# Three fillers between small on-chip buffers, in a post-norm transformer block

## The reference

```python
qkv = einsum('bsd,ed->bse', x, w_qkv) + b_qkv
scores = einsum('bhqd,bhkd->bhqk', q, k) / sqrt(32) + causal
out = einsum('bhqk,bhkd->bhqd', softmax(scores), v)
x = layernorm(x + einsum('bsd,ed->bse', out, w_out) + b_out)
Wg = (gate_w - 128) * gate_scale[:, None]        # Wu and Wd likewise
h = silu(einsum('bsh,ih->bsi', x, Wg)) * einsum('bsh,ih->bsi', x, Wu)
x = layernorm(x + einsum('bsi,hi->bsh', h, Wd))
```

## The kernel before, in words

| Buffers | Address modulo 256 |
|---|---|
| ident, x_tok, xT_hi, xT_lo, z_tok | 128 |
| w_stage; attT_hi, attT_lo, v_tok, q_sb, k_sb, wT_hi, wT_lo; hid_hi, hid_lo, gateT, upT, downT | 224 |
| inv_wide, attT | 160 |
| probs0 to probs3, probsT | 64 |

## Time and profile before

### The profile page before, as it was taken

How to read it: one execution, slowest core, us unless ns; L and a number is a source line. 1 busy time by engine, 2 the same in 40 slices (tenths; PEclk the granted TensorE clock), 3 DMA queues, 4 the chain that set the end, 5 groups by cost and what they waited for, 6 DMA issues and landing times.

```text
span 789.9 us, 11953 instructions
## 1 busy us (share of the span) xinstructions
PE 753.0 (95%) x4480; PEld 571.7 (72%) x4480; DVE 395.0 (50%) x1006; ACT 387.3 (49%) x914; POOL 128.3 (16%) x148
## 2 busy tenths in 40 slices
PE   7998899999999999999899999899999999999993
PEld 6776576776777676776578887688887888788882
DVE  3755666667567665667542222543226332453236
ACT  3754766666676666667646564422324222322220
POOL 0000111315131050302742233200000000000001
PEclk9999999999999999999999999899999999999997
DMA  9201422335422454312679944501110020000201
GB/s 315 85 1 28 134 60 74 81 81 139 149 62 59 115 149 134 81 37 52 138 131 196 265 146 146 175 14 40 67 54 0 13 82 11 0 1 27 80 1 55
DMA packets 59719, 68.67 MB, mean 87 GB/s; under 512 B 33552, under 2 KB 35600, under 8 KB 59536
## 3 DMA queue, kind: packets, MB, share of 16 engines
q1 hardware_dynamic: 53456, 49.05, 20.6%
q0 software_dynamic: 6208, 18.88, 10.3%
HBM read 59.53 MB, written 14.68 MB: 94 GB/s over the span
## 4 chain that ended last, share of the span: by engine, by line
PE 90%; DVE 4%; ACT 3%; issue 1%; DMA 1%; POOLq 0%; SPq 0%; POOL 0%; DVEq 0%; ACTq 0%
PE bank L1360 15%; PE bank L1361 15%; PE bank L1153 12%; PE bank L1229 9%; PE bank L1366 7%; PE bank L1367 7%; PE bank L1168 6%; PE bank L1212 5%; PE bank L1187 5%; PE bank L1250 5%; ACT probs L705 1%; DVE probs L912 1%; PE bank L1261 1%; PE bank L1115 1%; PE bank L1125 1%
## 5 line engine op out<-in xcount | busy, mean ns | idle before, releaser
L705 ACT ACTIVATE probs<-probs,neg_max 128x128 f32<-128x128 f32 (+3 forms) x256 | 140.5, 553 | 12.7 <-DVE neg_max L912 12.7
L1028 DVE SCALAR_TENSOR_TENSOR hid<-bank,u_scale,silu 128x512 f32<-128x512 f32 x64 | 48.1, 751 | 184.1 <-PE bank L1361 181.9
L912 DVE CUSTOM_DVE_ANT_0 probs<-bank,causal 128x128 f32<-128x128 f32 (+3 forms) x256 | 111.6, 484 | 29.1 <-PE bank L1212 27.7
L1360 PE MATMUL bank<-xT_hi,gateT 128*128 128x512 f32 x256 | 103.9, 406 | 5.3 <-DVE xT_lo L1037 3.5
L1361 PE MATMUL bank<-xT_lo,gateT 128*128 128x512 f32 x256 | 103.3, 403 | 0.0
L818 ACT ACTIVATE hid_hi<-hid 128x512 fp32r<-128x512 f32 x64 | 40.5, 632 | 126.2 <-DVE hid L1028 126.2
L1360 PE MATMUL bank<-xT_hi,upT 128*128 128x512 f32 x256 | 102.3, 400 | 0.0
L1361 PE MATMUL bank<-xT_lo,upT 128*128 128x512 f32 x256 | 101.9, 398 | 0.0
L1366 PE MATMUL bank<-downT,hid_hi 128*128 128x512 f32 x256 | 100.2, 391 | 0.9 <-DVE hid_lo L1031 0.8
L1367 PE MATMUL bank<-downT,hid_lo 128*128 128x512 f32 x256 | 99.7, 390 | 0.0
L1229 PEld LDWEIGHTS bank<-ident,probs 128*128 128x128 f32 x640 | 74.4, 144 | 30.5 <-issue 15.8
(11 more groups left out here) (94 smaller groups left out, 1138.3 us busy)
## 6 DMA issues: line engine op xcount, KB each, us to landing
scan_buf<-in_L_ffn_gate_w_dram SPq DMA_DIRECT2D x4, 1024.0 KB, 5.2
scan_buf<-in_L_ffn_up_w_dram SPq DMA_DIRECT2D x4, 1024.0 KB, 5.1
scan_buf<-in_L_ffn_down_w_dram SPq DMA_DIRECT2D x4, 1024.0 KB, 5.3
y_scratch<-z_tok SPq DMA_DIRECT2D x16, 256.0 KB, 4.6
x_tok<-y_scratch SPq DMA_DIRECT2D x4, 1024.0 KB, 6.5
w_int<-in_L_ffn_gate_w_dram POOLq DMA_DIRECT2D x16, 256.0 KB, 3.1
w_int<-in_L_ffn_up_w_dram POOLq DMA_DIRECT2D x16, 256.0 KB, 3.0
w_int<-in_L_ffn_down_w_dram POOLq DMA_DIRECT2D x16, 256.0 KB, 3.7
```

The lines of the kernel that those rows point to most:

```text
L705: nc.scalar.activation(probs[qb][:, j, :], probs[qb][:, j, :], ACT.Exp, bias=neg_max[:, qb, j:j + 1], scale=-1.0, accum_out=row_sum[:, qb, ...
L912: nc.vector.tensor_tensor_reduce(out=probs[qb][:, j, :], in0=score[j][:, first:first + w], in1=causal[:, S - w:S], scale=-SCALE, scalar=-F ...
L1028: nc.vector.scalar_tensor_tensor(out=hid[:, i % 2, :], in0=bank[:, :], scalar=u_scale[:, i:i + 1], in1=silu[:, i % 2, :], op0=ALU.mult, op ...
L1360: nc.tensor.matmul(acc[n][:, :], w[:, c, cols], form(xT_hi[:, c, :]), start=c == 0, stop=False)
```

## The change

Three buffers that nothing reads or writes are added. The first, of 160 bytes, stands behind the small buffers at the front and ahead of all that the stacks hold; the second, of 64 bytes, ahead of inv_wide; the third, of 96 bytes, ahead of probs0. No instruction is added, removed or moved on any engine, and no shape changes. Lines from 213 on have numbers that are higher by 1 to 5 afterwards.

```diff
+    LEVEL_FRONT, LEVEL_INVERSE, LEVEL_PROBS = 40, 16, 24
...
         minus_zero = sb("minus_zero", [P, 1])
+
+        sb("level_front", [P, LEVEL_FRONT])
...
         inv_sum = sb("inv_sum", [P, NT, HG], F32, att)
+        sb("level_inverse", [P, LEVEL_INVERSE], F32, att)
         inv_wide = sb("inv_wide", [P, NT, HG, HD], F32, att)
...
+        sb("level_probs", [P, LEVEL_PROBS], F32, att)
         P_WIDTH = [(qb + 1) * P for qb in range(NT)]
         probs = [sb(f"probs{qb}", [P, HG, P_WIDTH[qb]], F32, att) for qb in range(NT)]
```

## The result

| | before | after |
|---|---|---|
| first four runs of each, median us | 792.39 (790.03 to 793.28) | 780.42 (778.75 to 784.28) |
| ratio | | 0.986, 95% interval 0.9816 to 0.9905 |
| measured again later, median us | 789.85 (17 runs) | 782.26 (5 runs) |
| ratio | | 0.9908, 95% interval 0.9877 to 0.9940 |
| profiled execution, us | 792.13 | 784.28 |

Faster, as forecast. The profiled pair differs by 7.85 us, and 8.0 was forecast for it. Why these differences disagree, and how far 7.85 meets 8.0 by luck, is told with the experiments.

What follows compares the result with a forecast made beforehand. TensorE's matmul spacing was taken to bound the kernel. Gains of 7.0 + 0.6 + 0.6 = 8.2 us, less 0.2 for growing waits, gave 8.0 and a median of 785.1 us; range 781 to 791, its own case 781 to 787.5.

Steps and rivals of the forecast that it cites:

- What bounds the kernel: Whole kernel: TensorE (PE), busy 753.0 of 789.9 us, bounds it; its waits, 23.5 us, should stay within 0.3 us.
- Gate, up and down (the front filler): Feed-forward part: operands equal modulo 256 bring gate and up from 233.8 to 226.4 ns each; with down, 7.0 us gained.
- settling: Gate and up: after batch starts and transposes of y, 12 times 10 matmuls stay slow, taking 0.9 us off the gain.
- V, Q and K: Attention projections, in short blocks: equal operands gain 0.6 us in V and 0.6 us in Q and K.
- The two small fillers: Attention, probs and inv_wide: equality gives transposes nothing, so 0 was taken; the weighted values' upper bound was 1.3 us.
- Waits that grow: Where PE waits for other work, as for hid, the waiting grows; 0.2 us was taken off the gain.
- The total: Whole kernel: 8.0 us gained, the profiled execution from 792.1 to 784.1 us, the median of runs at 785.1.
- Addresses have nothing to do with it: Rival for the slow matmul pairs: something of xT other than its address; no change, 793.1 us, chance 0.09.
- a start at 128 is what costs: Rival: an operand at address 128 modulo 256 is slow by itself; 3.9 us slower, 797.0 us, chance 0.06.
- Half of it: Rival: first steps after each switch between gate, up and down stay slow; gain about 4 us, 789 us, chance 0.09.

Runs made afterwards that it cites:

- runs of 48: Separate kernel without the block's work: 48 float32r matmuls of 512 columns back to back per operand distance; 226.7 ns each at 0, 232.5 to 234.4 at 96.
- all at 224: The full change plus 96 more bytes ahead of ident, so every TensorE operand is at address 224 modulo 256; 782.29 us, ratio 0.9903.

## Why the prediction was right

**What bounds the kernel.** Right: PE was busy for 753.0 us and is for 744.8, and the span shrank with it from 789.9 to 782.1. Its waits grew by 0.4 us in total.

**Gate, up and down (the front filler).** 7.0 us were forecast, and 7.3 came once waits and clock are taken out: 7.0 in gate and up, where 6.5 were forecast, and 0.35 in down in place of 0.5. The spacing fell to the 227 ns named. The term that was sized a little too dear is settling: 10 matmuls at full loss were taken for each of 12 interruptions (0.9 us), but behind the transposes of y the timeline of the kernel after shows that they settle sooner in some places:

```profile
476.12 0.47 PE L1365 MATMUL bank<-xT_hi,gateT 128*128 128x512 f32 x1
476.44 0.39 PE L1366 MATMUL bank<-xT_lo,gateT 128*128 128x512 f32 x1
...
478.05 0.39 PE L1365 MATMUL bank<-xT_hi,upT 128*128 128x512 f32 x1
...
479.86 0.39 PE L1371 MATMUL bank<-downT,hid_hi 128*128 128x512 f32 x1
```

The 8 steps from 478.05 to 479.86 take 226 ns each, so all is settled by the ninth matmul.

**V, Q and K.** 0.6 + 0.6 us were forecast. From the transposes of the inverse sums in one group to those in the next, the 13 groups without a change of clock gained between 0.02 and 0.11 us each, 1.0 us in sum. Matmul by matmul, over all of attention, Q and K gained 0.7 us in both traces of the change, V 0.5 and 0.6, and the output projection, for which nothing was forecast, 0.2 and 0.0. So how a block of V or of the output projection settles varies between two executions of one kernel, and the 0.06 and 0.03 us per 24 of the rows above aren't fixed sizes. For Q and K the number came out by a way other than argued: 0.6 was 1.0 less what the wait for ScalarE's exponentials would grow by, but that wait stayed at 3.4 us, and the matmuls gained 1.8 ns each and not 2.5. Two errors cancel there.

**The two small fillers.** Forecast 0, measured 0 (1.0016, with 1 in the interval). In the full change too, all transposes and all weighted values of attention together differ by under 0.1 us from before.

**Waits that grow.** 0.2 us were forecast. The wait for hid grew from 1.8 to 1.9, that for xT_lo was between 3.2 and 4.1 us in the kernels with the front filler and 3.5 before: within what varies.

**The total.** 7.3 + 1.0 = 8.3 us by the traces, 8.2 to 8.4 by the runs at like clock, 8.0 forecast. The median missed 785.1 by more. The forecast was set on the three runs of before at hand, with a median of 793.1; the 17 later ones had 789.9, though their mean clock of 0.984 was about that of the profiled execution (0.983). So the base was some 3 us too high for what came later. The traces show 1.7 to 2.6 us of this at the start of the kernel; the prediction had no term for it, and its low bound of 781 left no room for it: the first median fell 0.6 below.

**The rivals.** "Addresses have nothing to do with it" fell with the runs of 48, "a start at 128 is what costs" with all at 224. "Half of it" fell, since gate and up have 227 ns from the first matmul of a step. The Trainium skill says in "TensorE: Matmul & The Clock Gate", section "Step-by-step: what each phase is for", that loading the next weights takes no read bandwidth from the running matmul. The prediction drew from it that no pair of addresses costs anything; that holds in the bfloat16 runs here (215.8 ns at three distances) and not in those in float32r (226.7 to 234.4 ns). Whether it is the weight load that costs the time there, no run shows.

What stays open is the cause. That the weight load of the next matmul and the moving operand of the running one meet in SBUF would fit most of the above, also that alternate weights give half the loss, but no run separated the two reads; it is a guess and not shown. It doesn't explain why 240 and 252 are fast and 244 and 248 are not, nor why with 256 columns the equal pair is the slower one.

## What to carry to other kernels

Where a kernel is bound by long runs of float32r matmuls of 512 columns, read the start-to-start distance of each kind of matmul in the timeline, not its duration. If kinds of one shape differ by some 3%, compare the addresses of their two operands modulo 256; a small buffer between the large ones can undo it, here at a price of 160 bytes. In blocks of six between other work it brings only 1 to 2.5 ns a matmul, against 7 in long runs. Measure such a gain in the traces, at equal clock, since the runs of one kernel differ by as much as the gain.

## What the hardware showed that was not expected

- The spacing of matmuls of one shape at 2.4 GHz runs from 226.7 to 234.4 ns with nothing changed but the distance between the operands' addresses. Unequal pairs go round in a fixed pattern: 231, 232 and 237 ns in turn for V.
- With 256 columns the equal pair is the slower one: 120.0 against 117.4 ns.
- Bfloat16 operands showed no dependence at the three distances tried, at 215.8 ns.
- A fast pair can be settled at once (distance 256 right behind 240, and 240 right behind 224) or need up to 11 matmuls (V's block of 16 in the kernel after, both at 96 behind -96); what ran before has a part in it, so that equal operands in a kernel speed up their neighbours too, and unequal ones slow them down (down's 8 matmuls: 1.81 us behind equal pairs, 1.82 and 1.84 behind pairs 96 and 192 apart).
